# Scores ahead of transposes: reordering the cross-attention loop of a perceiver layer

## The reference

```python
q = (xn @ Wq);  k = (cn @ Wk);  v = (cn @ Wv)        # cn: 257 context rows of 384 per sequence
sim = einsum('bhid,bhjd->bhij', q, k) * scale
attn = softmax(sim, axis=-1)
x = x + einsum('bhij,bhjd->bhid', attn, v) @ Wo
```

## Time and profile before

| | us |
|---|---|
| median of 3 runs (1530.2 to 1531.81) | 1530.48 |
| profiled execution | 1530.54 |
| its span, first to last instruction | 1528.6 |
| PE busy | 1441.0 (94%) |
| PE weight loads busy (beside PE) | 898.9 (59%) |
| DVE busy | 669.8 (44%) |
| ACT busy | 446.0 (29%) |
| POOL busy | 113.7 (7%) |

### The profile page before, as it was taken

One profiled execution on the slowest core, in us unless ns is written; L12 is line 12 of the kernel. 1 busy time (PEld: TensorE's weight loads), 2 busy tenths in 40 slices (PEclk: granted clock), 3 DMA queues, 4 the chain that ended last, 5 costly groups with the idle time before them and its releaser, 6 DMA issues.

```text
span 1528.6 us, 22267 instructions
## 1 busy us (share of the span) xinstructions
PE 1441.0 (94%) x7517; PEld 898.9 (59%) x7518; DVE 669.8 (44%) x1694; ACT 446.0 (29%) x917; POOL 113.7 (7%) x168
## 2 busy tenths in 40 slices
PE   6899999999999999999839999999999999999997
PEld 5677686776868777686624444444444444444442
DVE  5755848567585765847342311211121121122115
ACT  3535536254362634536101111111111111111100
POOL 1000010100001001000100000000000000000005
PEclk9999999999999999999969999999999999999998
DMA  9650100001010000100166165225060516000005
GB/s 364 256 214 11 34 14 23 33 10 31 14 31 24 21 21 16 39 15 1 55 242 261 33 249 204 76 84 204 14 268 18 208 69 268 21 14 21 14 7 172
DMA packets 42811, 140.34 MB, mean 92 GB/s; under 512 B 3366, under 2 KB 3476, under 8 KB 37660
## 3 DMA queue, kind: packets, MB, share of 16 engines
q0 software_dynamic: 16256, 83.89, 14.4%
q1 hardware_dynamic: 26496, 56.03, 10.5%
q10 hardware_dynamic: 28, 0.01, 0.0%
HBM read 110.55 MB, written 29.36 MB: 92 GB/s over the span
## 4 chain that ended last, share of the span: by engine, by line
PE 87%; DVE 6%; issue 3%; ACT 2%; POOL 1%; DMA 0%; ACTq 0%; DVEq 0%; SPq 0%; POOLq 0%
PE bank L549 21%; PE bank L567 21%; PE bank L1266 8%; PE bank L1224 7%; PE bank L1187 4%; PE bank L1292 4%; PE bank L1208 3%; PE bank L1280 3%; PE bank L559 3%; PE bank L1233 2%; PE bank L1314 2%; PE bank L1348 2%; PE bank L1248 2%; DVE moe_w L970 2%; PE bank L1267 1%
## 5 line engine op out<-in xcount | busy, mean ns | idle before, releaser
L549 PE MATMUL bank<-moe_w,arena 128*128 x736 | 332.9, 595 | 2.3 <-POOL pool_mark L357 2.3
L567 PE MATMUL bank<-moe_w,arena 128*128 x736 | 330.9, 592 | 0.0
L461 DVE TENSOR_TENSOR arena<-bank,arena 128x512 f32<-128x512 f32 x92 | 63.6, 692 | 478.2 <-PE bank L549 478.2
L549 PEld LDWEIGHTS bank<-moe_w,arena 128*128 128x128 f32 x736 | 140.5, 191 | 179.1 <-issue 179.1
L399 ACT ACTIVATE arena<-arena 128x512 f32<-128x512 f32 x92 | 57.9, 630 | 579.2 <-DVE arena L461 579.2
L567 PEld LDWEIGHTS bank<-moe_w,arena 128*128 128x128 f32 x736 | 132.7, 190 | 132.5 <-issue 132.5
L1224 PE MATMUL bank<-moe_w 128*128 128x257 f32 x768 | 188.7, 383 | 6.4 <-DVE moe_w L770 6.4
L1224 PEld LDWEIGHTS bank<-moe_w 128*128 128x128 f32 x768 | 137.2, 190 | 25.4 <-DVE moe_w L770 5.8
L1266 PE MATMUL bank<-moe_w 128*128 128x512 f16 x384 | 114.5, 379 | 9.9 <-ACT moe_w L827 7.0
L813 ACT ACTIVATE moe_w<-bank,cols,ugain 128x512 f32<-128x512 f32 x96 | 74.5, 777 | 61.7 <-PE bank L1267 60.7
L970 DVE TENSOR_TENSOR moe_w<-bank,moe_w 128x512 f16<-128x512 f32 (+1 forms) x96 | 65.5, 689 | 48.0 <-ACT moe_w L827 45.6
(11 more groups left out here) (196 smaller groups left out, 1613.3 us busy)
## 6 DMA issues: line engine op xcount, KB each, us to landing
moe_w<-in_L_ffn_w_dram POOLq DMA_DIRECT2D x16, 4096.0 KB, 19.5
xs_rows<-blocks SPq DMA_DIRECT2D x8, 2048.0 KB, 12.8
arena<-in_ctx_dram SPq DMA_DIRECT2D x32, 384.0 KB
arena<-in_L_ffn_b_dram POOLq DMA_DIRECT2D x8, 1024.0 KB, 26.6
arena<-xs_rows SPq DMA_DIRECT2D x23, 256.0 KB, 2.7
ys_rows<-arena SPq DMA_DIRECT2D x23, 256.0 KB, 2.1
moe_w<-in_L_xattn_Wq_dram SPq DMA_DIRECT2D x1, 2048.0 KB, 8.1
moe_w<-in_L_xattn_Wo_dram SPq DMA_DIRECT2D x1, 2048.0 KB, 18.2
```

Source lines behind the costliest of these rows:

```text
L461: nc.vector.tensor_tensor(h_sb[:, fb % 2, :], bank[fb % 2][:, :], b1_rows[:, bass.ds(slot * FF + fb * 512, 512)], ALU.add).then_inc(h_bias ...
L549: last = nc.tensor.matmul(bank[fb % 2][:, :], xsT[:, k, :], moe_flat[:, bass.ds((e % 2) * 16384 + k * FF + fb * 512, 512)], start=(k == 0) ...
L567: last = nc.tensor.matmul(Y[:, :], hT_sb[:, fb % 2, c, :], moe_flat[:, bass.ds((e % 2) * 16384 + 8192 + (4 * fb + c) * DIM, DIM)], start=( ...
```

## The change

Two loops change, one in PE's program and one in DVE's. On PE, in batches 1 to 3, the transposes of part k come after the scores of head k + 1, no longer after those of head k. On DVE, the maximum of head k comes first, and the low half of part k - 1 after it, no longer the low half of part k and then the maximum of head k. ACT's order is unchanged.

```diff
@@ DVE body @@
                     for k in range(HG):
                         if do_a:
-                            if b >= 1 and k < 3:
-                                pt_lo(g, b - 1, k)
                             row_max(g, b, k)
+                            if b >= 1 and k >= 1:
+                                pt_lo(g, b - 1, k - 1)
                         if do_b and b == 3:
                             if k == 0:
                                 ss_sum(g - 1)
@@ PE body @@
                         if do_a and b == 0 and h < 3:
                             ct_fill(tp(g, ("ct", 1, h)), GB * g + 1, 1, h)
-                        if do_a and b >= 1 and h < 3:
-                            pt_fill(g, b - 1, h)
+                        if do_a and b >= 1 and h >= 1:
+                            pt_fill(g, b - 1, h - 1)
```

## The result

| | before | after |
|---|---|---|
| median of 4 runs, us | 1530.34 (1529.84 to 1531.81) | 1566.41 (1564.77 to 1569.94) |
| profiled execution / its span, us | 1530.54 / 1528.6 | 1564.77 / 1562.8 |
| PE busy, us | 1441.0 | 1444.0 |

The ratio after to before is 1.0237, 95% interval 1.0217 to 1.0257: slower by 36 us. The forecast was 1564, range 1551 to 1572.

What follows compares the result with a forecast made beforehand. TensorE, busy 94% of the span, was taken as the bound. Batch 2's 10.4, batch 1's 5.6 and batch 3's 0.85 and 16.8 summed to 33.7 us on 1530.5, giving 1564 us, range 1551 to 1572.

Steps and rivals of the forecast that it cites:

- Batch 2: Second changed batch: the last score no longer covers cast and low half, costing 1.30 us in each of 8 groups, 10.4.
- The 0.16 us wait of the earlier trace: Batch 2 before the change: the context transpose's wait for the last low half, read as a chain only just hidden.
- Batch 1: First changed batch: one wait goes and two come late, costing 0.7 us in each of 8 groups, 5.6.
- p2 has a second wait: Batch 1: the last transposes (p2) also need the first low half, held behind heads_apart and now two maxima costing 0.7.
- The wait for L962: Batch 1: PE's first transposes wait for the normalised probabilities, 6.5 us over 8 groups; forecast to go, 0.9 won.
- lower bound of 0.4: Batch 1's least cost per group, from PE's own order: 1.30 less the 0.9 won.
- Batch 3: Third changed batch: late casts and DVE's softmax queue delay the product, 2.4 us in seven groups, 0.85 in the first.
- the third pair: Batch 3: the product's last matmuls, needing the last two low halves; forecast to start at 448.1, where it was 445.69.
- The first group: Group without self-attention work: forecast at 0.7 in batch 1, 1.30 in batch 2 and 0.85 in batch 3.
- Clock, 1588: Case listed among the chances: the clock matters and the time is 1588 us; chance 0.03.
- Casts only: Rival: only casts and the TP bank count, batch 3's DVE queue being in time; 1553 us, chance 0.14.
- Faster: Rival: the L962 wait goes in every group and other PE work hides what was covered; 1524 us, chance 0.02.

Runs made afterwards that it cites:

- PE's order alone: Only the PE half of the diff, with DVE's order of the kernel before: 1551.51 us, 1.0134 of before.
- batch 2 alone: The change made on both engines in batch 2 only, batches 1 and 3 as in the kernel before: 1540.99 us, 1.0067 of before.
- A version that does: Kernel before with heads_apart behind batch 1's maxima and PE's batch 1 reordered, one score kept behind the last transposes: 1522.19 us, 0.9949 of before.
- the heads_apart move: Kernel before with heads_apart on DVE moved from ahead of batch 1's maxima to behind them, nothing else: 1527.79 us, 0.9976 of before.

## Why the prediction was right

- **Range and sign.** 1566.4 lies in 1551 to 1572, 2.4 above the forecast, and the chance of slower was 0.96.
- **Batch 2** was forecast at 1.30 and costs 1.31, in the profile after and alone in 93.23 - 91.91 = 1.32. The 0.16 us wait of the earlier trace rows was the sign to read: a path already just uncovered gives no slack.
- **Batch 1** was forecast at 0.7 and costs 0.78; the step "p2 has a second wait" holds: PE's order alone costs 0.00 there, and moving heads_apart takes 0.95 off the group. The wait for L962 went, as said. Its lower bound of 0.4 (1.30 less the 0.9 won) was wrong: p2 had been held once more before, and by the forecast's own count it was due at 417.0 without lo0, no later than its 417.09 before. With heads_apart out of the way batch 1 wins 0.15.
- **Batch 3** was forecast at 2.4 for the seven groups and costs 1.96. The mechanism holds (the softmax moved: 1.18 back), the size was off in two places: the third pair was put at 438.30 + 9.8 and came 466.44 - 456.92 = 9.52 us after s0. The softmax's sum came 0.1 sooner than put (L861 starts 0.49 behind the cast's start, not 0.58), and the operations behind it took 461.31 to 466.44, 5.1 where 5.3 was put, since on DVE too one starts before the recorded end of the last. And 0.17 is given back later, which the sum left out. The wait before the product, put at about 0.9, is 0.67, and the one before the third pair 1.10, not 1.5.
- **The first group** was forecast at 0.7 + 1.3 + 0.85 = 2.85 and costs 4.33, of which the low clock is 1.6: 2.7.
- **The clock** is where a step failed. It was held at 1.00 in the forecast. The case "Clock, 1588" of the chances puts 24 us on the forecast for falls of the clock; no run shows such a term: it fell in few groups, 1.57 each, and by the account above adds about 5 us to the median. The 1.00 was read from a mean over 735 us, which reads 1.00 after the change as well and hides a fall to 0.50 at 755 us in the kernel before; and it rested on one execution, in which the wait of 2.61 us in the first group left the clock at 1.00, while the same wait came with stretches at 0.53 in the traces of batch 2 alone and of PE's order alone. The 0.76 of 765 to 772 us wasn't the only low reading there either: 755.0 to 761.7 and 768.7 to 782.0 both read 0.50. The sum of the orders was 33.7 where they cost 31, and the clock, left out, adds 5: the two errors partly cancel, and that the forecast came nearer than its parts is luck.
- **The rivals.** Casts only (1553) falls by the wait of 1.10 before the third pair. Faster falls: this order doesn't keep the cover. A version that does is 8 us faster than before, 3 of them by the heads_apart move alone.

## What to carry to other kernels

Before moving work on one engine ahead of a wait, ask what that work was covering behind it: the path through the other engines that starts at the moved step is then paid in full (1.31 us in batch 2, where the score that went ahead takes 1.30). Here waits of 0.16 and 0.17 us that end on another engine were the mark of such a path. And the order of a partner engine's queue has to move with it, but only where it shortens that path: here the maxima ahead of the low halves cost 28.7 us alone and 15 on top of PE's order, and a copy left behind on ScalarE cost a finished gain of 8 us. Last, a mean clock over 735 us read 1.00 with two falls of 3.4 us to 0.51 in it: read it in windows not much longer than what is looked for.

## What the runs showed of the hardware

Waits of 0.7 to 3.9 us on TensorE in this loop can be followed by, and in some first groups end in, a stretch of 3.4 us (in some first groups 6.8) at a granted clock of 0.50 to 0.57 in the windows above, in some executions and groups and not in others of the same kernel. Between the first group and the end of the last they were seen only behind two waits about 2.1 us apart, of 0.65 to 0.72 and 1.39 to 1.47 us in batch 1 or of 0.67 to 0.72 and 1.10 to 1.16 us in batch 3, and not behind every such pair. A stretch cost 1.57 to 1.68 us where PE was busy, about half of it. Runs of one kernel differ with their mean clock, by 5 us after (1564.77 at 0.980 to 1569.94 at 0.974) and by 3.4 us in 19 runs of before (1529.09 at 0.981 to 1532.47 at 0.979); that such stretches are all of it is argued, since few runs have a trace.

From start to start DVE and ACT can be faster than the recorded durations: DVE starts a maximum 0.61 us behind the start of a subtraction recorded as 0.69, and ACT starts L861 0.49 behind the start of a cast recorded as 0.59 (460.16 to 460.65 after). So the sum of durations overrated the queue of batch 3: the forecast added up 5.64 us from L999 to the end of lo2, and the trace after has 466.38 - 461.31 = 5.07.
